# Relation passes: TensorE fetches 24 of 52 columns by quarters, with one-hots from ScalarE

## What is computed

```python
def rgcn_conv(x, src, dst, edge_type, W, root, bias):
    x_src = x[src]                                   # one row of 16 values per edge
    msg = zeros
    for r in range(8):
        msg += where(edge_type == r, x_src @ W[r], 0)
    norm = 1 / max(count(dst, edge_type), 1)
    agg = segment_sum(msg * norm, dst)
    return agg + x @ root + bias
```

## Time and profile before

| | us |
|---|---|
| median of three runs | 29117.51 |
| profiled execution, first to last instruction (span) | 27450.7 |
| median less span | 1666.8 |
| TensorE matmul busy in the span | 22119.0 (81%) |
| VectorE busy | 19222.1 (70%) |
| GpSimd busy | 16809.7 (61%) |
| ScalarE busy | 4820.0 (18%) |
| first relation pass | 8193 to 11534 |
| second relation pass | 11805 to 14936 |

### The profile page before, as it was taken

The page is one execution under the profiler, slowest core; times in us unless marked ns, Lnnn a source line. Parts: engine busy times, 40 slices in busy tenths (PEclk is TensorE's granted clock), DMA queues, the critical chain, the costliest instruction groups (busy, mean ns, idle before and its releaser), DMA issues. The chain is left out here.

```text
span 27450.7 us, 471355 instructions
## 1 busy us (share of the span) xinstructions
PE 22119.0 (81%) x173244; PEld 18663.0 (68%) x173244; DVE 19222.1 (70%) x43784; ACT 4820.0 (18%) x6981; POOL 16809.7 (61%) x15348
## 2 busy tenths in 40 slices
PE   0788849888849999789996688898888885488886
PEld 0677734444438888678886588888888885277775
DVE  4799965555547777667775466666666665599997
ACT  0555520000000000000000011111111111244443
POOL 1555556666645555556555388887887888444444
PEclk9999969999969999889998899999999997699998
DMA  5222211111111111111111222222222222522221
GB/s 81 70 74 74 74 40 39 40 40 39 40 31 32 34 34 34 26 37 32 33 31 24 31 35 36 37 35 39 35 39 35 39 35 24 142 68 63 67 63 47
DMA packets 1643238, 1254.71 MB, mean 46 GB/s; under 512 B 1250266, under 2 KB 1485204, under 8 KB 1599476
## 3 DMA queue, kind: packets, MB, share of 16 engines
q0 software_dynamic: 854944, 176.35, 10.5%
q1 hardware_dynamic: 676628, 617.76, 8.0%
q10 hardware_dynamic: 110016, 437.07, 4.2%
HBM read 764.42 MB, written 465.15 MB: 45 GB/s over the span
## 5 line engine op out<-in xcount | busy, mean ns | idle before, releaser
L954 PE MATMUL gat_e_found<-gat_e_parts,gat_e_lowhot 128*128 128x462 bf16 (+1 forms) x27528 | 5590.9, 366 | 957.4 <-DVE gat_e_rows L919 813.1
L2425 PE MATMUL sheaf_e_found<-sheaf_e_parts,sheaf_e_lowhot 128*128 128x238 bf16 x46872 | 5322.1, 275 | 989.5 <-DVE sheaf_e_lowhot L2237 456.9
L2186 POOL DMA_INDIRECT bysrc<-sheaf_e_toadd,sheaf_e_torow x3224 | 5170.4, 1604 | 1393.0 <-issue 784.7
L2425 PEld LDWEIGHTS sheaf_e_found<-sheaf_e_parts,sheaf_e_lowhot 128*128 128x128 bf16 x46872 | 4712.2, 102 | 1446.2 <-issue 622.8
L954 PEld LDWEIGHTS gat_e_found<-gat_e_parts,gat_e_lowhot 128*128 128x128 bf16 (+1 forms) x27528 | 3790.8, 142 | 2757.0 <-DVE gat_e_rows L919 944.5
L1073 POOL DMA_INDIRECT gat_e_rows<-att_t,gat_e_index x4216 | 4005.5, 950 | 2498.3 <-DMA gat_e_rows<-att_t,gat_e_index 1276.1
L751 POOL DMA_INDIRECT rgcn_e_rows<-rel_t,rgcn_e_index x3968 | 3749.0, 945 | 2842.1 <-DMA rgcn_e_rows<-rel_t,rgcn_e_index 1512.4
L1916 PEld LDWEIGHTS rgcn_e_found<-rgcn_e_parts,rgcn_e_lowhot 128*128 128x128 bf16 x52080 | 5030.0, 99 | 544.8 <-issue 485.7
L1916 PE MATMUL rgcn_e_found<-rgcn_e_parts,rgcn_e_lowhot 128*128 128x224 bf16 x52080 | 5233.5, 263 | 74.8 <-issue 69.3
L2880 POOL DMA_INDIRECT typed_e_rows<-typed_t,typed_e_index x1736 | 1655.5, 954 | 1720.8 <-DMA typed_e_rows<-typed_t,typed_e_index 724.3
L954 PE MATMUL typed_e_found<-typed_e_parts,typed_e_lowhot 128*128 128x400 f32 x11904 | 2440.8, 359 | 44.3 <-DVEq L2770 44.3
(11 more groups left out here) (500 smaller groups left out, 26436.9 us busy)
## 6 DMA issues: line engine op xcount, KB each, us to landing
sheaf_e_allsrc<-src_d ACTq DMA_DIRECT2D x62, 1664.0 KB
typed_e_types<-in_type_t SPq DMA_DIRECT2D x62, 1536.0 KB
sumsatt<-gat_e_sums ACTq DMA_DIRECT2D x62, 1404.0 KB
rgcn_e_low<-low_d SPq DMA_DIRECT2D x124, 640.0 KB
typed_t<-typed_p_y SPq DMA_DIRECT2D x98, 765.0 KB
sheaf_e_low<-low_d SPq DMA_DIRECT2D x62, 1152.0 KB, 8.5
sumsatt<-gat_e_sums ACTq DMA_DIRECT2D x62, 1092.0 KB
gat_e_rows<-att_t,gat_e_index POOLq DMA_INDIRECT x4216
```

The lines of the kernel that those rows point to most:

```text
L954: last = pe.matmul(self.found_ps[n % 2][:, c, 0:self.width * self.cut.highs], hot[:, k, col * P:(col + 1) * P], self.table.column(part, k) ...
L2186: pool.indirect_dma_start(g.by_src[k][r], rows(to_row[k][:, j:j + 1]), to_add[k][:, j, 0:FD], None, compute_op=ALU.add).then_inc(summed[k] ...
L2425: last = pe.matmul(found_ps[n % 2][:, c, 0:W * NHI], hot[:, k, col * P:(col + 1) * P], short.column(part, k), start=part == 0 and k == 0, ...
```

## The change

NPE goes from 20 to 24: six steps of four columns by matmul, and 28 gathers. In both passes the table h is cut by `quarters`: the low part is under 512 (four tiles), the high part has 25 values (FHI), and h is held in two float32r parts. A step's found matmuls are 4 x 4 x 2 = 32 of 400 columns. As 400 float32 fill most of a PSUM bank, a step needs four banks, and `found_ps` becomes two buffers of two columns each, in place of two of four columns: the first half of every step uses the one, the second half the other. `lifted` counts the halves that VectorE has multiplied out, and each half of a step waits for that half of the step before. `pick` becomes `lift`, two instructions. The low one-hots move from VectorE to ScalarE: Abs of the difference, then Relu of one less it. VectorE's order in a step is now `weigh`, `lift`, `gather_kinds`, `take`.

```diff
-NPE = 20
+NPE = 24
-        short = SplitTable(s, sevenths(g), [h[:, :, :]], FD)
+        short = SplitTable(s, quarters(g), [h[:, :, :]], FD)
-        found_ps = [s.ps(f"found{k}", [P, QC, 256]) for k in range(2)]
+        found_ps = [s.ps(f"found{n}", [P, 2, 512]) for n in range(2)]
...
+                def lift(G, k, q, fresh=False):
                     if not fresh:
                         dve.wait_ge(taken, G)
+                    for n in range(2):
+                        dve.wait_ge(found, 2 * G + n + 1)
+                        j = q * QC + 2 * n
+                        dve.tensor_tensor(picked[:, 2 * n:2 * n + 2, :, :],
+                                          found_ps[n][:, :, 0:FHI * FD].rearrange("p c (f h) -> p c f h", h=FHI),
+                                          high_hot[k][:, j:j + 2, :].unsqueeze(2).to_broadcast([P, 2, FD, FHI]),
+                                          ALU.mult).then_inc(lifted, 1)
...
                     if not (begin and at < 3):
                         weigh(o, G - 3, k3, q3)
                     if not (begin and at < 1):
-                        pick(o, G - 1, k1, q1, fresh=begin and at < 2)
-                    if not end:
-                        nk, nq = ((at + 1) % (2 * NQ)) // NQ, (at + 1) % NQ
-                        build_low(G + 1, i + 1 if at == 2 * NQ - 1 else i, nk, nq, fresh=begin and at < 1)
-                    if not (begin and at < 1):
-                        dve.wait_ge(dve_o, o.base + o.n)
-                        take(o, G - 1, at - 1, fresh=begin and at < 3)
+                        lift(G - 1, k1, q1, fresh=begin and at < 2)
                     if not (begin and at < 3):
                         gather_kinds(o, G - 3, k3, q3)
+                    if not (begin and at < 1):
+                        take(G - 1, at - 1, fresh=begin and at < 3)
...
                     pe.wait_ge(low_built, G + 1)
-                    if not (begin and at < 2):
-                        pe.wait_ge(taken, G - 1)
                     for c in range(QC):
-                        for n in range(NLO):
-                            for part in range(3):
-                                last = pe.matmul(found_ps[at % 2][:, c, 0:NHI * FD],
+                        if c % 2 == 0 and not (begin and at < 1):
+                            pe.wait_ge(lifted, 2 * G - 1 + c // 2)
+                        for n in range(FLO):
+                            for part in range(2):
+                                last = pe.matmul(found_ps[c // 2][:, c % 2, 0:FHI * FD],
                                                  low_hot[at % 2][:, n, c * P:(c + 1) * P], short.column(part, n),
-                                                 start=n == 0 and part == 0, stop=n == NLO - 1 and part == 2)
-                    last.then_inc(found, 1)
+                                                 start=n == 0 and part == 0, stop=n == FLO - 1 and part == 1)
+                        if c % 2 == 1:
+                            last.then_inc(found, 1)
...
+                def build_low(G, turn, k, q, fresh=False):
...
+                    for n in range(FLO):
+                        last = act.activation(away[:, n, :], low[k][:, q * QC * P:(q + 1) * QC * P], ACT.Abs,
+                                              bias=g.low_f[:, n:n + 1], scale=-1.0)
+                    last.then_inc(away_ready, 1)
+                    act.wait_ge(away_ready, G + 1)
+                    if not fresh:
+                        act.wait_ge(found, 2 * G - 2)
+                    act.activation(low_hot[(k * NQ + q) % 2][:, :, :], away[:, :, :], ACT.Relu, bias=1.0, scale=-1.0)\
+                        .then_inc(low_built, 1)
...
+                            if not (end and at == 2 * NQ - 1):
+                                nk, nq = ((at + 1) % (2 * NQ)) // NQ, (at + 1) % NQ
+                                build_low(i * (2 * NQ) + at + 1, i + 1 if at == 2 * NQ - 1 else i, nk, nq,
+                                          fresh=begin and at < 1)
```

More of the change, by code:

```diff
@@ L1761, in _, with take @@
                 short.split(dve, o)
[L1763 to L1767, removed]
-                    for n in range(NLO):
[L1769 to L1773, removed]
+                def lift(G, k, q, fresh=False):
                     if not fresh:
                         dve.wait_ge(taken, G)
[L1776 to L1782, removed]
+                    for n in range(2):
[5 more added lines that the diff above has]
+                                          ALU.mult).then_inc(lifted, 1)
+                def take(G, at, fresh=False):
+                    dve.wait_ge(lifted, 2 * G + 2)
                     if not fresh:
@@ L1805, in prepare @@
                     o.step(dve.tensor_tensor(high_hot[k][:, :, :],
[L1806 to L1807 removed]
+                                             count_ps[:, 0:FHI].unsqueeze(1).to_broadcast([P, NPE, FHI]),
+                                             high[:, JP:].unsqueeze(2).to_broadcast([P, NPE, FHI]), ALU.is_equal))
                     some = slice(0 if first else JP, J)
@@ L1848, in finish, with step @@
                     dve.wait_ge(b.done[k], i + 2)
-                def step(o, i, k, q, begin=False, end=False):
+                def step(o, i, k, q, begin=False):
                     G = i * (2 * NQ) + k * NQ + q
@@ L1872, in turn @@
                         for q in range(NQ):
-                            step(o, i, k, q, begin, end and k == 1 and q == NQ - 1)
+                            step(o, i, k, q, begin)
                             if q == 2 and not (begin and k == 0):
@@ L1878, in drain @@
                     G = G_END
-                    pick(o, G - 1, 1, NQ - 1)
+                    lift(G - 1, 1, NQ - 1)
                     weigh(o, G - 3, 1, NQ - 3)
-                    dve.wait_ge(dve_o, o.base + o.n)
-                    take(o, G - 1, 2 * NQ - 1)
+                    take(G - 1, 2 * NQ - 1)
                     gather_kinds(o, G - 3, 1, NQ - 3)
@@ L1887, in drain @@
                     finish(o, NCH // 2 - 1, 1)
-                build_low(0, 0, 0, 0, fresh=True)
                 turn(o, 0, begin=True)
-                base, per = o.n, 2 * ((5 if first else 4) + 2 * NQ + 1)
+                base, per = o.n, 2 * ((5 if first else 4) + NQ + 1)
                 with dve.Fori(1, NCH // 2 - 1) as i:
@@ L1895, in _ @@
                 o = Order(dve, dve_o, (NCH // 2 - 2) * per + base)
-                turn(o, NCH // 2 - 1, end=True)
+                turn(o, NCH // 2 - 1)
                 drain(o)
@@ L1963, in copy_turned, with turn @@
                     act.copy(h_col[at % 2][:, :], turned_ps[0:QC * FD, :]).then_inc(copied, 1)
-                def turn(i, begin=False):
+                def build_low(G, turn, k, q, fresh=False):
+                    if q == 0:
+                        act.wait_ge(low_in[k], turn * 16 + 16)
+                    if not (fresh and q == 0):
+                        act.wait_ge(low_built, G)
+                    for n in range(FLO):
[7 more added lines that the diff above has]
+                        .then_inc(low_built, 1)
+                def turn(i, begin=False, end=False):
                     for k in range(2):
-                        if first:
-                            act.wait_ge(norm_ready[k], i + 1)
-                            act.dma_start(chunk(norm_d, i, k), norm[k][:, :]).then_inc(norm_stored[k], 16)
                         for q in range(NQ):
                             at = k * NQ + q
+                            if not (end and at == 2 * NQ - 1):
+                                nk, nq = ((at + 1) % (2 * NQ)) // NQ, (at + 1) % NQ
+                                build_low(i * (2 * NQ) + at + 1, i + 1 if at == 2 * NQ - 1 else i, nk, nq,
+                                          fresh=begin and at < 1)
+                            if first and q == 1:
+                                act.wait_ge(norm_ready[k], i + 1)
+                                act.dma_start(chunk(norm_d, i, k), norm[k][:, :]).then_inc(norm_stored[k], 16)
                             if not (begin and at < 1):
@@ L1975, in turn @@
                                 b.store_chunk(act, acc, i - 1 + k, 1 - k)
+                build_low(0, 0, 0, 0, fresh=True)
                 turn(0, begin=True)
-                with act.Fori(1, NCH // 2) as i:
+                with act.Fori(1, NCH // 2 - 1) as i:
                     turn(i)
+                turn(NCH // 2 - 1, end=True)
                 copy_turned(G_END - 1, 2 * NQ - 1)
```

37 lines of the change are left out of this document (20 added, 17 removed).

## The result

The changed kernel takes 30180.49 us, the median of four runs (30161.71 to 30213.26), against 29107.11 us of four runs of the kernel before beside it. The ratio is 1.0371, with a 95% interval of 1.0356 to 1.0386: 3.7% slower, a loss of 1073 us. I had forecast a loss of 1623 us. Measured again beside later runs, the ratio was 1.0386 (1.0369 to 1.0403).

What follows compares the result with a forecast made beforehand. TensorE, 94 and 96% busy, was taken to bound the relation passes; 13.3 and 13.0 us more a chunk over 62 chunks gave +1631, about +1620 with the h saving. Span 29070 plus 1666.8 outside it made 30740 us, range 30050 to 31250.

Steps and rivals of the forecast that it cites:

- The wait: Before a step's first found matmuls: TensorE idles 1.8 us for the first lift, queued behind weigh; restart at 3.06 us.
- The matmuls: Found matmuls on TensorE: 32 spaced 0.188 us take 6.03 us; with the wait a step takes 9.09 us.
- The preparation: VectorE's chunk preparation delays the next lift: TensorE idles 3.8 us more a chunk in the second pass, 6.9 in the first.
- The clock: TensorE's granted clock falls after the new idle time in one step of two, costing 5.5 us a chunk.
- The sum for the passes: Both relation passes: chunks of 63.8 us in the second and 66.9 in the first, +1631 us over 62 chunks each.
- The saving of 8 us a pass in splitting h: Splitting h into two parts of four tiles, not three of seven, saves some 8 us a pass, an estimate.
- The number it is set against: Timed median of before stands 1666.8 us above the profiled span; claimed to lie outside the instructions and stay unchanged.
- A: Rival: the lift before the found matmuls is hidden, TensorE steps take 7.29 us; about 29100 or 28250 us; chance 0.06.
- B: Rival: TensorE's clock holds in short idle times, only the step behind the preparation is slow; 30360 us; chance 0.21.
- C: Rival: TensorE's clock falls every step, +10 us a chunk; 31110 us, or 31700 with mostly long falls; chance 0.17.

Runs made afterwards that it cites:

- third profile of before: The kernel before, unchanged, profiled once more beside the run with fewer gathers: 29151 us, with a span of 29149.5 us.
- first profile: The kernel before, unchanged, as profiled ahead of the change: span 27450.7 us, where the median of its timed runs was 29117.5 us.
- the reordered version: The changed kernel with lift moved ahead of weigh in VectorE's order of a step: 28347 us, ratio 0.9876 against the kernel before.

## Why the prediction was right, and where it was not

**The wait.** Right in place and size: restart 3.07 us after the transpose where I had 3.06, idle time 1.75 where I had 1.75 to 1.8, weigh at 1.43, the sum of 1600 elements 1.81 us. Exchanging two lines took it away.

**The matmuls.** A spacing of 0.188 us and a step of 9.0 us at full clock against 9.09.

**The preparation.** The sum had it take 3.8 and 6.9 us more from TensorE. In the second pass the step behind it is 13.6 us, 4.6 over a 9.0 step with the low clock's part in it; TensorE's idle time there is 3.97 us, 2.2 more than the 1.75 of the other steps, since the slow step ahead is 1.6 us longer and hides that much. The term was right only together with the clock's.

**The clock.** Mis-sized: I took one step in two, since six of 13 idle stretches of 1.35 to 1.50 us had been followed by the low level and 20 of 30 of about 2 us. In the second pass it is nearly all steps but the one behind the histogram; in the first, 55 to 90% of the three that follow that one, and all of the others. 5.5 us a chunk was forecast; the median chunk of 64.85 less my 58.3 makes 6.5.

**The sum for the passes.** 66.9 and 63.8 us a chunk were forecast, 67.5 and 64.85 measured. The passes of the changed kernel came within 1% of what I had (6517 and 1631 make 8148, against 8226). The saving of 8 us a pass in splitting h was an estimate that no run measures by itself.

**The number it is set against.** This step of the prediction failed: "that is outside the first and last instruction and stays". The difference of 1666.8 us between the median of the runs and the profiled span was 6% of the kernel, and it was inside: 646 us of it in the two passes that the change touches. The third profile of before spends 520 us in breaks inside its trains of 84 matmuls, and its GpSimd waits 933 us for the finish in the two passes where the first profile has 201; the changed kernel has two breaks. So the change gained some 550 us that the first profile did not show, and the loss is 1073 and not 1623. That the time still fell in the range was luck in part: its lower end, 30050, had been set by a clock that doesn't fall at all, and the clock fell in nearly every step. The room was meant for another error than the one that was made. Had I asked what a gap of 1667 us can be, when nothing of the kernel runs outside its first and last instruction, the term would have been a range and not a constant.

**The rivals.** A, the hidden lift, did not come; it is what the reordered version shows, whose 51.4 and 54.6 us compare with my 50.5 and 53.6. B gave 30360, and 30060 with no fall at all. These are the nearest numbers, by accident: the clock did fall. C was the truer picture of the clock, but its numbers don't follow from its own words: 10 us more a chunk make 31290, above the end of the range; 31110 comes out only if 1.5 us of it are hidden ahead of the preparation, which C doesn't say.

## What to carry to other kernels

When two buffers that held a whole step each become the halves of one, look at what stands ahead of the instruction that frees them in its engine's queue; if that waits for the other engine's last work of the step, the two run in turns, and exchanging the two lines is worth more than the change itself. Price a new idle time of TensorE with its low clock too, for every step. Hold the profiled span against the timed runs before building on it: where they differ by more than the effect in question, profile again.

## What was not expected of the hardware

TensorE's trains break, often two or three times close together, some 1.2 us in all (520 us in 439 groups of breaks), with no releaser in the profile: about 500 us in 5200 us of found matmuls, in two profiles of before and not in a third. All breaks of these two profiles, and all 591 of the run with fewer gathers, begin within 2.5 us of the start of a gather on GpSimd. The changed kernel, with found matmuls 0.188 us apart, has two; with the long work of VectorE spread it has 174.

A loop turn with 1376 matmuls and weight loads of TensorE stays loaded (11 packets in a pass), one with 1844 is loaded again every turn (275 or 276 packets), and that by itself made no breaks.

And 0.95 us of matmuls of zeros in an idle time of 1.75 us kept the clock at 2.4 GHz: the 32 matmuls behind it took 6.10 us and not 7.65.
